# Softmax sums of fourteen heads in four column groups, and one reciprocal a head spread over the partitions through DRAM

## The chip, the cores and the metric

The kernel runs on all 8 cores of one Trainium2 chip. Each core does the same work on its own half of one of the four sequences. The metric is the time on the device in microseconds (us) of the slowest core; lower is better.

## What is computed

One transformer layer: attention with 16 heads of 128 columns over a sequence of 2048, a residual and a layer norm, then a feed-forward net of 8192 hidden columns, again with residual and layer norm. The part that the change touches is the softmax and its normalisation:

```python
q = (x @ Wq.T + bq).reshape(b, s, h, dh) * jnp.cos(rot)
k = (x @ Wk.T + bk).reshape(b, s, h, dh) * jnp.sin(rot)
v = (x @ Wv.T + bv).reshape(b, s, h, dh)
scores = jnp.einsum('bshd,bthd->bhst', q, k) / np.sqrt(dh) * spiral_weight[None, :, None, None]
attn = jax.nn.softmax(scores, axis=-1)
out = jnp.einsum('bhst,bthd->bshd', attn, v).reshape(b, s, d)
x = _layernorm(x + out @ Wo.T + bo)
x = _layernorm(x + gelu(x @ proj1.T + b1) @ proj2.T + b2)
```

Each core has 1024 queries (its half of the sequence) and all 2048 keys.

## The kernel before

Each engine has its own program, written out by hand, and the programs meet in semaphores. `H`, `X` and `W` are large tiles in SBUF in which named slices live; `ps` is all of PSUM, eight banks of 512 f32 columns, and `pair` is two double banks that the score steps use in turn.

The attention stage is a loop over 16 heads h with 16 steps tc each, one step for every 128 keys. In a step TensorE computes the scores of 128 keys against the 1024 queries into one `pair` (L658), then a share of projection matmuls as filler (L460 for k, L464 for q of the next head, L469 for v; `jobs(h)` is how many of these jobs of 16 matmuls a head has: 10 in heads 0 and 8 to 12, 9 in heads 1, 2 and 4 to 7, 8 in head 3, 7 in head 13, 5 in head 14), then the product of the exponentials of the step before with v (`p_v`, L607). ScalarE takes the exponential out of `pair` (L874) into one of three buffers, and VectorE adds it into `acc` (L1042). So `acc` holds, for each query, 128 partial sums, one on each partition; after the last step VectorE splits it into two bf16 halves, `hl` (L1057, L1059).

The sum over the partitions is `denom`, in step 2 of the next head: four matmuls with a stationary matrix of ones of 128 columns (L617), so that the total of each query comes out on every one of the 128 partitions. ScalarE copies this 128x1024 block to `rec` (`denom_out`, L852), VectorE takes its reciprocal in four pieces of 256 columns (`recip`, L993) in steps 3 to 6, and multiplies the head's output `avraw` with it in step 7 (`normalise`, L998). With two semaphores around it: TensorE goes on to step 4 of a head only when `a_den` tells that the copy is done, and ScalarE overwrites `avraw` at the start of the next head only when `d_norm` tells that the multiplication is done.

In step 12 of a head (13 in heads 3 and 13; `norm_step`) the bound of the next head's scores is worked out. TensorE adds squares in `norm_sums` (L479, L482), eight matmuls whose stationary matrix is 32 columns wide and which go to four groups of 32 partitions. VectorE takes maxima (`norm_pick`, L972 to L976) and sets `d_nsel`; TensorE spreads them one step later (`norm_all`, L489, which waits for `d_nsel`), VectorE multiplies (`norm_out`, L981, L986, sets `d_nprod`), TensorE waits for that before the scores of the step after, and GpSimd makes `neg_b` from it (L392, L394), which ScalarE needs for the next head's first exponential.

GpSimd issues all weight loads, with a conversion from f32 to bf16 under way (`load`, L371). Its program has a pass for each head h, which runs while TensorE is in head h-1: it waits for `pe_k`, loads wk for head h+2, waits for `pe_q`, loads wq for head h+1, waits for `d_nprod`, makes `neg_b`. Some passes end with loads of their own: pass 1 and 9 four slabs of wv, pass 12 and 13 four slabs of wo (`won`), pass 14 six slabs of wo, after it has waited for `pe_k` to reach 64, which is after the third job of head 14. SyncE moves the residual through DRAM meanwhile (`xpieces`, `xbo_scr`).

After the heads come the product with wo (L725), layer norm, the two products of the feed-forward net (L744, L755; L784, L800) and the last layer norm, whose statistics are in the tiles `ln_st`.

Of the kernel before, what the change touches and what calls it, by code (L numbers as in the profile page):

```python
# [89 lines left out]
def build():  # L90
# [15 lines left out]
    consts = nc.dram_tensor("consts", [128, 68], F32, kind="ExternalInput").ap()  # L106
    xbo_scr = nc.dram_tensor("xbo_scr", [1024, 2048], F32, kind="Internal").ap()
    x1_scr = nc.dram_tensor("x1_scr", [1024, 2048], F32, kind="Internal").ap()
    r2_scr = nc.dram_tensor("r2_scr", [1024, 512], F32, kind="Internal").ap()
    out = nc.dram_tensor("out", [1024, 2048], F32, kind="ExternalOutput").ap()  # L110

    with contextlib.ExitStack() as ctx:
# [15 lines left out]
        b2_bc = sbuf("b2_bc", [128, 2048], F32)  # L128

        bo_bc = sbuf("bo_bc", [128, 2048], F32)  # L130
        ln_st = [sbuf(f"ln_st{i}", [128, 24 if i < 7 else 30], F32) for i in range(8)]
        ln_mv = [sbuf(f"ln_mv{i}", [128, 2], F32) for i in range(8)]
        ln_cols = sbuf("ln_cols", [128, 24], F32)
        ln_sd, ln_rs, ln_nm = [[ln_cols[:, k * 8 + i:k * 8 + i + 1] for i in range(8)]
# [76 lines left out]
        s_bo = sem("s_bo")  # L211
        s_bv = [sem("s_bv0"), sem("s_bv1")]
        s_b2 = sem("s_b2")
        s_xt = [sem(f"s_xt{i}") for i in range(8)]
        s_x = [sem(f"s_x{i}") for i in range(16)]
        s_xp = [sem("s_xp0"), sem("s_xp1")]
# [31 lines left out]
        d_trig, d_const, d_v = sem("d_trig"), sem("d_const"), sem("d_v")  # L248
        d_nsel, d_nprod = sem("d_nsel"), sem("d_nprod")
        d_acc, d_hl, d_norm = sem("d_acc"), sem("d_hl"), sem("d_norm")  # L250
        d_xbo, d_r1 = sem("d_xbo"), sem("d_r1")
        d_mv1, d_x1bf = sem("d_mv1"), sem("d_x1bf")
        d_r2, d_mv2, d_nm2 = sem("d_r2"), sem("d_mv2"), sem("d_nm2")
# [114 lines left out]
        @block.gpsimd  # L368
        def _(e):
            def load(dst, src, done):  # L370
                e.dma_start(out=dst, in_=src, max_dma_last_dim=8192).then_inc(done, 16)  # L371

            for g in range(4):
                load(H[:, half(g, 2048)], xtc[g], s_x[g])
                load(wslab[2 + g], wvc[g], s_wv[g])
                load(H[:, half(4 + g, 2048)], xtc[4 + g], s_x[4 + g])
                load(wv1[g], wvc[4 + g], s_wv1[g])
            load(wk[0], wkt[0], s_wk[0])
            load(wslab[1], wqt[0], s_wq)
            for i in range(8, 16):  # L380
                load(H[:, half(i, 2048)], xtc[i], s_x[i])
            load(wk[1], wkt[1], s_wk[1])
            for h in range(16):
                if h < 15:
                    if h < 14:
                        e.wait_ge(pe_k, 4 * (h + 1))
                        load(wk[h % 2], wkt[h + 2], s_wk[h % 2])
                    e.wait_ge(pe_q, 2 * (h + 1))
                    load(wslab[1], wqt[h + 1], s_wq)

                e.wait_ge(d_nprod, h + 1)
                e.tensor_tensor(nroot[:], nprod[:], half_sb[:], ALU.pow).then_inc(g_root, 1)  # L392
                e.wait_ge(g_root, h + 1)
                e.tensor_single_scalar(neg_b[:, h:h + 1], nroot[:], -1.0,  # L394
                                       ALU.mult).then_inc(g_negb, 1)


                if h == 1:
                    e.wait_ge(pe_v, 24)
                    for g in range(4):  # L400
                        load(wslab[2 + g], wvc[8 + g], s_wv[g])
                if h == 9:
                    e.wait_ge(pe_v, 48)
                    for g in range(4):
                        load(wslab[2 + g], wvc[12 + g], s_wv[g])
                if h == 12:
                    e.wait_ge(pe_av, 192)
                    for d in range(4):
                        load(wo_sb[d], won[d], s_wo[d])
                if h == 13:  # L410
                    e.wait_ge(pe_v, 64)
                    for d in range(4, 8):
                        load(wo_sb[d], won[d], s_wo[d])
                if h == 14:
                    e.wait_ge(pe_k, 64)
                    for d in range(8, 14):
                        load(wo_sb[d], won[d], s_wo[d])
            e.wait_ge(pe_q, 32)
            for d in range(14, 16):
                load(wo_sb[d], won[d], s_wo[d])  # L420

            def slab(n, src):
                load(wslab[ring(n)], src, s_w[ring(n)])

            for n in range(2):
                slab(n, p1t[n])
            e.wait_ge(pe_av, 256)
            for i in range(2):
                load(p1_own[i], p1t[2 + i], s_own[i])
            e.wait_ge(pe_wo, 32)  # L430

            e.wait_ge(s_xt[7], 16)
            for n in range(4, 64):

                if 8 <= n < 10:
                    e.wait_ge(pe_f1, n - 7)
                elif n >= 10:
                    e.wait_ge(pe_f1, n - 5)
                slab(n, p1t[n])
            for n in range(60):  # L440
                if n < 6:
                    e.wait_ge(pe_f1, 59 + n)
                else:
                    e.wait_ge(pe_p2, n - 5)
                slab(G_P2 + n, p2n[n // 16][n % 16])
                if n == 57:

                    e.wait_ge(pe_p2, 52)
                    for i in range(4):
                        load(p2_late[i], p2n[3][12 + i], s_wl[i])  # L450
            for s in range(8):
                e.wait_ge(d_nm2, s + 1)
                e.tensor_scalar(r2[2][s], r2[2][s], ln_rs[s][:], ln_nm[s][:],
                                ALU.mult, ALU.add).then_inc(g_out, 1)
# [3 lines left out]
        def _(t):  # L458
# [153 lines left out]

            def denom(h, dst):
                t.wait_ge(d_hl, h + 1)
                for sc in range(2):
                    for part in range(2):
                        ins = t.matmul(dst[:, half(sc, 512)], ones_sq_sb[:],  # L617
                                       hl[:, half(2 * part + sc, 512)],
                                       start=(part == 0), stop=(part == 1))
                ins.then_inc(pe_den, 1)  # L620
# [185 lines left out]
        def _(a):  # L806
# [42 lines left out]

            def denom_out(h, src):  # L850
                a.wait_ge(pe_den, h + 1)
                a.activation(out=rec if h < 15 else rec15, in_=src, func=AF.Copy).then_inc(a_den, 1)  # L852


            a.wait_ge(d_v, 16)
# [76 lines left out]
        def _(v):  # L932
# [61 lines left out]

            def normalise(h):
                v.wait_ge(a_av, h + 1)
                v.drain()
                v.tensor_mul(pool_a[h], avraw if h < 15 else avraw15,  # L998
                             rec if h < 15 else rec15).then_inc(d_norm, 1)
# [28 lines left out]
            for h in range(16):  # L1028
                for tc in range(16):
                    n = 16 * h + tc  # L1030
                    if tc == norm_step(h) and h < 15:
                        norm_pick(h + 1, pair[(turn(h, tc) + 1) % 2])
                    if tc == norm_step(h) + 1 and h < 15:
                        norm_out(h + 1, pair[(turn(h, tc - 1) + 1) % 2])
                    if tc == 1:
                        v.wait_ge(a_exp, n + 1)
                        v.drain()
                        v.tensor_add(acc, pbuf[(n - 1) % 3], pbuf[n % 3]).then_inc(d_acc, 2)
                    if tc > 1:
                        v.wait_ge(a_exp, n + 1)  # L1040
                        v.drain()
                        v.tensor_add(acc, acc, pbuf[n % 3]).then_inc(d_acc, 1)  # L1042
                    if 0 < h < 15 and 3 <= tc <= 6:
                        recip(h - 1, tc - 3)
                    if 0 < h < 15 and tc == 7:
                        normalise(h - 1)
                    if 0 < h < 12 and tc in (1, 8, 10) and (h, tc) != (11, 10):
                        if h == 1 and tc == 1:
                            v.wait_ge(s_bo, 16)
                        add_bo(3 * h - 3 + (1, 8, 10).index(tc))  # L1050
                    for j in range(jobs(h)):
                        kind, c, blk = job(h, j)
                        if job_ends(h, j) == tc and kind == "v":
                            v_out(c, blk, JOB_BANK[kind, c, blk])
                    if tc == 15:
                        v.drain()
                        v.tensor_copy(hl[:, half(0)], acc)  # L1057
                        v.drain()
                        v.tensor_sub(hl[:, half(1)], acc, hl[:, half(0)]).then_inc(d_hl, 1)  # L1059
# [32 lines left out]
            for p in range(4):  # L1092
                r_p = r2a if p == 0 else r2[p]
                for s in range(8):
# [29 lines left out]
                    if p == 3:  # L1124
                        if s == 0:
                            v.wait_ge(s_r2r, 128)
                        v.drain()
                        v.bn_aggr(ln_mv[s][:], ln_st[s][:]).then_inc(d_mv2, 1)  # L1128
                        v.wait_ge(a_sd2, s + 1)
                        v.reciprocal(ln_rs[s][:], ln_sd[s][:])  # L1130
                        v.drain()
# [81 lines left out]
```

## Time and profile before

| | us |
|---|---|
| median of 3 runs | 1829.99 (1829.6 to 1830.45) |
| the profiled execution | 1830.17 |
| its span, slowest of 8 cores (core 5) | 1828.3 |
| spans of the 8 cores | 1825.9 to 1828.3 |
| TensorE busy | 1798.1 (98%) |
| VectorE busy | 711.5 (39%) |
| ScalarE busy | 536.4 (29%) |
| GpSimd busy | 143.4 (8%) |

The span is the time from the first to the last instruction of the core; a little lies around it. In the profile PE is TensorE (matmuls), PEld its weight loads, DVE VectorE, ACT ScalarE, POOL GpSimd, SP SyncE. A group or row names the line of the kernel, what it writes and reads (`out<-in`, without buffer numbers), and how often. A matmul's own duration (379 ns for 512 columns) is longer than the time that it takes in the stream, since matmuls are pipelined; the distance from one start to the next is what it costs. In brackets stands the idle time before an instruction and what ended it.

### The profile page before, as it was taken

Reading aid. Unit: us, or ns where it says so; the run is one execution under the profiler, and the core shown is the slowest. Engines: PE = TensorE matmul, PEld = TensorE weight load, DVE = VectorE, ACT = ScalarE, POOL = GpSimd, SP = SyncE. Lnnn points to the kernel's source line nnn. Section 1 sums busy time; section 2 is a strip of 40 time slices with the busy share of each in tenths; the row PEclk is TensorE's granted clock in tenths of the full one; section 3 lists DMA queues with packets and bytes.
Section 4 is the critical chain, followed back from the end, with each engine's and each line's share of the span. In section 5 each row is a group of like instructions: output and inputs, shape, how many; then the busy total and the mean of one; then the engine's idle time right before and its main releaser. Section 6 shows DMA issues by size and latency. Waiting matters only on the chain.

```text
span 1828.3 us, 22539 instructions; the slowest of 8 cores (1825.9 to 1828.3 us)
## 1 busy us (share of the span) xinstructions
PE 1798.1 (98%) x8448; PEld 814.5 (45%) x8448; DVE 711.5 (39%) x841; ACT 536.4 (29%) x539; POOL 143.4 (8%) x252
## 2 busy tenths in 40 slices
PE   6999999999999999999999999999999999999997
PEld 2444444444444444434444444444444444444444
DVE  5436777777666666688620000000000030210315
ACT  0135556555555555672211111111110000000001
POOL 3001000000000011010000000000000000000011
PEclk9999999999999999999999999999999999999999
DMA  9934323223253324375876544545544485565776
GB/s 162 161 71 76 61 56 67 55 56 61 59 99 60 53 38 62 57 115 152 230 165 112 81 73 77 79 73 80 75 75 70 75 161 88 95 106 76 156 128 177
DMA packets 70889, 172.45 MB, mean 94 GB/s; under 512 B 22912, under 2 KB 22912, under 8 KB 68480
## 3 DMA queue, kind: packets, MB, share of 16 engines
q0 software_dynamic: 29952, 109.07, 39.4%
q1 hardware_dynamic: 39680, 59.85, 12.6%
q10 hardware_dynamic: 1152, 2.10, 0.5%
q8 instruction: 71, 1.16, 0.3%
q14 instruction: 34, 0.28, 0.1%
HBM read 248.58 MB, written 27.26 MB: 151 GB/s over the span
## 4 chain that ended last, share of the span: by engine, by line
PE 97%; DMA 1%; ACT 1%; DVE 0%; issue 0%; DVEq 0%; POOL 0%; ACTq 0%; POOLq 0%
PE ps L784 24%; PE ps L755 23%; PE ps L469 12%; PE ps L460 12%; PE ps L464 6%; PE ps L607 6%; PE ps L658 6%; PE ps L725 5%; PE ps L744 2%; PE ps L627 1%; PE ps L617 1%; DMA W<-wvc 1%; ACT X L874 0%; PE ps L800 0%; DVE X L1042 0%
## 5 line engine op out<-in xcount | busy, mean ns | idle before, releaser
L755 PE MATMUL ps<-X,W 128*128 128x512 bf16 x1920 | 414.6, 379 | 0.0
L784 PE MATMUL ps<-W,H 128*128 128x512 bf16 x1904 | 412.1, 379 | 0.0
L874 ACT ACTIVATE X<-ps,neg_b 128x1024 bf16<-128x1024 f32 x256 | 284.5, 1112 | 242.1 <-PE ps L658 232.6
L1042 DVE TENSOR_TENSOR X<-X 128x1024 f32<-128x1024 f32 x224 | 274.4, 1225 | 180.1 <-ACT X L874 169.9
L755 PEld LDWEIGHTS ps<-X,W 128*128 128x128 bf16 x1920 | 187.8, 98 | 226.6
L784 PEld LDWEIGHTS ps<-W,H 128*128 128x128 bf16 x1904 | 186.3, 98 | 224.6
L1121 DVE TENSOR_TENSOR X<-ps,bo_bc 128x512 f32<-128x512 f32 x24 | 16.6, 691 | 662.0 <-PE ps L784 660.3
L469 PE MATMUL ps<-W,H 128*128 128x512 bf16 x768 | 188.9, 382 | 15.3 <-DMA W<-wvc 15.3
L917 ACT ACTIVATE H<-ps,b_sb 128x1024 bf16<-128x1024 f32 x64 | 71.3, 1114 | 353.1 <-PE ps L755 347.6
L607 PE MATMUL ps<-X,H 128*128 128x512 bf16 x512 | 152.2, 379 | 2.0 <-ACT X L874 1.7
L658 PE MATMUL ps<-X 128*128 128x512 bf16 x480 | 142.7, 379 | 0.5 <-DVE nprod L986 0.4
L464 PE MATMUL ps<-H,W 128*128 128x512 bf16 x512 | 130.3, 379 | 0.0
L460 PE MATMUL ps<-H 128*128 128x512 bf16 x512 | 129.6, 379 | 0.0
L460 PE MATMUL ps<-H,W 128*128 128x512 bf16 x512 | 127.8, 379 | 0.0
L469 PEld LDWEIGHTS ps<-W,H 128*128 128x128 bf16 x768 | 74.7, 99 | 105.9 <-issue 21.6
L921 ACT ACT_TABLE_LOAD x1 | 1.3, 1283 | 394.5 <-DVE ln_mv L1128 394.5
L993 DVE RECIPROCAL X<-X 128x256 f32<-128x256 f32 x60 | 104.3, 1743 | 0.0
L817 ACT ACTIVATE X<-ps,bks,sinv 128x512 bf16<-128x512 f32 x60 | 46.5, 775 | 110.2 <-PE ps L460 110.2
L607 PEld LDWEIGHTS ps<-X,H 128*128 128x128 bf16 x512 | 49.4, 98 | 64.8 <-issue 6.7
L464 PEld LDWEIGHTS ps<-H,W 128*128 128x128 bf16 x512 | 50.1, 98 | 60.4
L460 PEld LDWEIGHTS ps<-H,W 128*128 128x128 bf16 x512 | 50.1, 98 | 60.4
L460 PEld LDWEIGHTS ps<-H 128*128 128x128 bf16 x512 | 50.1, 98 | 60.0 <-issue 0.3
(119 smaller groups left out, 1081.4 us busy)
## 6 DMA issues: line engine op xcount, KB each, us to landing
W<-p1t POOLq DMA_DIRECT2D x62, 512.0 KB, 5.9
W<-p2n POOLq DMA_DIRECT2D x60, 512.0 KB, 8.5
H<-xtc POOLq DMA_DIRECT2D x16, 512.0 KB, 50.7
W<-wqt POOLq DMA_DIRECT2D x16, 512.0 KB, 7.8
xpieces<-xn SPq DMA_DIRECT2D x32, 256.0 KB, 3.9
xbo_scr<-xpieces SPq DMA_DIRECT2D x32, 256.0 KB, 4.3
H<-xbo_scr SPq DMA_DIRECT2D x8, 1024.0 KB, 7.1
x_scr<-H SPq DMA_DIRECT2D x8, 1024.0 KB, 4.9
```

The source lines that it names most:

```text
L460: return t.matmul(bank[b], wk[h % 2][:, half(i, 128)], x_t(c, i), start=(i == 0), stop=(i == 15))
L464: return t.matmul(bank[b], wslab[1][:, half(i, 128)], x_t(c, i), start=(i == 0), stop=(i == 15))
L469: return t.matmul(bank[b], x_t(blk // 4, i)[:, half(blk % 4, 128)], w[:, half(i % 4, 512)], start=(i == i0), stop=(i == i1 - 1))
L607: ins = t.matmul(bank[4 + sc], v_blk(h // 4, tc)[:, half(h % 4, 128)], pbuf[n % 3][:, half(sc, 512)], start=(tc == 0), stop=(tc == 15))
L658: ins = t.matmul(pair[k % 2][:, half(sc, 512)], kbuf[h][:, half(tc, 128)], qbuf[h % 2][:, half(sc, 512)], start=True, stop=True)
L725: ins = t.matmul(bank[(s % 2) * 4 + c], pool_a[d][:, half(s, 128)], wo_sb[d][:, half(c, 512)], start=(d == 0), stop=(d == 15))
L755: ins = t.matmul(bank[b0 + c], wslab[ring(ho)][:, half(i, 128)], X[:, i * 1024 + c * 512:i * 1024 + (c + 1) * 512], start=(i == 0), stop=( ...
L784: ins = t.matmul(bank[s], hid[k][:, half(s, 128)], w[:, half(i, 512)], start=(k == 0), stop=(k == (31 if p == 3 and s == 7 else 63)))
L874: a.activation(out=pbuf[n % 3], in_=pair[turn(h, tc) % 2], func=AF.Exp, bias=neg_b[:, h:h + 1]).then_inc(a_exp, 1)
L917: a.activation(out=hid[ho], in_=ps[:, half(ho % 4)], func=AF.Gelu, bias=b1_sb[:, ho:ho + 1]).then_inc(a_gelu, 1)
L993: v.reciprocal(r[:, half(i, 256)], r[:, half(i, 256)])
L1042: v.tensor_add(acc, acc, pbuf[n % 3]).then_inc(d_acc, 1)
```

## The change

The sums of the heads 0 to 13 are computed another way; heads 14 and 15 stay as they were. `denom` now gives eight matmuls of 256 columns with a stationary matrix of 32 columns: the queries 256c to 256c+255 are summed into the partitions 32c to 32c+31, first for one half of `hl`, then for the other. So each total stands on 32 partitions and not on 128, and the block is 128x256. ScalarE copies this block into a new tile `rec4`. VectorE takes one reciprocal of it, in step 3, and sets `d_rec`.

GpSimd waits for that at the top of its pass h, from pass 2 on, for the reciprocals of head h-2. It issues a write of one row of each group (partitions 0, 32, 64, 96; 4 rows of 1 KB) to a DRAM tensor `rec_scr`, waits until it has landed, and issues a read of these 4 KB, broadcast to all 128 partitions, into `rec` (512 KB). `normalise` waits for this transfer (`s_rec`) and is moved from step 7 to step 11. The statistics `ln_st` of the layer norms, which were tiles of their own, now lie in `rec4`.

```diff
+        rec4 = sbuf("rec4", [128, 256], F32)
+        ln_st = [rec4[:, i * 24:i * 24 + (24 if i < 7 else 30)] for i in range(8)]
...
             for h in range(16):
+
+                if h >= 2:
+                    e.wait_ge(d_rec, h - 1)
+                    e.dma_start(out=rec_scr[:], in_=rec4[0:128:32, :]).then_inc(s_rst, 16)
+                    e.wait_ge(s_rst, 16 * (h - 1))
+                    e.dma_start(out=rec, in_=rec_scr.rearrange("a b -> (a b)").unsqueeze(0)
+                                .to_broadcast([128, 1024])).then_inc(s_rec, 16)
                 if h < 15:
                     if h < 14:
                         e.wait_ge(pe_k, 4 * (h + 1))
...
             def denom(h, dst):
                 t.wait_ge(d_hl, h + 1)
+                if h < 14:
+
+                    for part in range(2):
+                        for c in range(4):
+                            ins = t.matmul(dst[32 * c:32 * c + 32, 0:256], ones_sq_sb[:, 0:32],
+                                           hl[:, half(4 * part + c, 256)],
+                                           start=(part == 0), stop=(part == 1))
+                    ins.then_inc(pe_den, 1)
+                    return
...
             def denom_out(h, src):
                 a.wait_ge(pe_den, h + 1)
-                a.activation(out=rec if h < 15 else rec15, in_=src, func=AF.Copy).then_inc(a_den, 1)
+                if h < 14:
+                    a.activation(out=rec4[:], in_=src[:, 0:256], func=AF.Copy).then_inc(a_den, 1)
+                else:
+                    a.activation(out=rec if h < 15 else rec15, in_=src,
+                                 func=AF.Copy).then_inc(a_den, 1)
...
             def normalise(h):
                 v.wait_ge(a_av, h + 1)
+                if h < 14:
+                    v.wait_ge(s_rec, 16 * (h + 1))
                 v.drain()
...
-                    if 0 < h < 15 and 3 <= tc <= 6:
-                        recip(h - 1, tc - 3)
-                    if 0 < h < 15 and tc == 7:
+                    if 0 < h < 15 and tc == 3:
+                        v.wait_ge(a_den, h)
+                        v.reciprocal(rec4[:], rec4[:]).then_inc(d_rec, 1)
+                    if 0 < h < 15 and tc == 11:
                         normalise(h - 1)
```

## Rows read from the trace of the kernel before

**Rows 1.** The page's first part: busy us (share), instructions.

```profile
PE 1798.1 (98%) x8448; PEld 814.5 (45%) x8448; DVE 711.5 (39%) x841; ACT 536.4 (29%) x539; POOL 143.4 (8%) x252
```

**Rows 2.** Windows, head 14: length, PE, PEld, DVE, ACT, POOL busy; PEclk, DMA share, GB/s.

```profile
769.30:806.00 36.70, 34.62 (x165) 15.24 (x164) 28.52 (x27) 25.09 (x28) 4.67 (x8) 1.00 0.48 75
```

**Rows 3.** TensorE's waits in the span: us in total, times, longest us.

```profile
PE ps L469 <- DMA W<-wvc: 15.3, 1, 15.3
```

**Rows 4.** Timeline of TensorE, the sums in head 1: start us, us, what.

```profile
163.23 1.03 PE L617 MATMUL ps<-b_bc,ones_sq_sb 128*128 128x512 bf16 x4
164.09 0.38 PE L460 MATMUL ps<-H,W 128*128 128x512 bf16 x1
```

**Rows 5.** Timeline of TensorE, norm_sums in step 12 of head 1.

```profile
191.72 0.59 PE L658 MATMUL ps<-X 128*128 128x512 bf16 x2
192.24 0.40 PE L479 MATMUL ps<-b_bc,ones_sq_sb 128*32 128x512 bf16 x4
192.47 0.28 PE L482 MATMUL ps<-X,ones_sq_sb 128*32 128x256 bf16 x4
192.69 1.04 PE L469 MATMUL ps<-H 128*128 128x512 bf16 x4
```

**Rows 6.** Groups by line, each shape apart: busy us, mean ns, idle before.

```profile
L993 DVE RECIPROCAL X<-X 128x256 f32<-128x256 f32 x60 | 104.3, 1743 | 0.0
L998 DVE TENSOR_TENSOR H<-X 128x1024 bf16<-128x1024 f32 x15 | 18.4, 1225 | 1.4
```

**Rows 7.** Timeline, all engines: nsel and norm_all of heads 1 and 11.

```profile
194.11 0.22 DVE L976 TENSOR_SCALAR nsel<-consts_sb,nmax 128x4 f32<-128x4 f32 x1
...
195.50 0.28 PE L489 MATMUL ps<-nsel,onesf_sb 128*128 128x8 f32 x2
...
668.00 0.23 DVE L976 TENSOR_SCALAR nsel<-consts_sb,nmax 128x4 f32<-128x4 f32 x1
...
669.61 0.28 PE L489 MATMUL ps<-nsel,onesf_sb 128*128 128x8 f32 x2
```

**Rows 8.** Timeline of GpSimd in head 14: the loads that end pass 14.

```profile
786.45 3.25 POOL L371 DMA_DIRECT2D H<-won  x6 [16.85 <-PE ps L460]
```

**Rows 9.** The page's third part: packets, MB and share of the software queue.

```profile
q0 software_dynamic: 29952, 109.07, 39.4%
```

**Rows 10.** DMA issues of 786.4 to 786.9 and 789.1 to 789.7: median us to landing.

```profile
H<-won POOLq DMA_DIRECT2D x1, 512.0 KB, 6.8
...
H<-won POOLq DMA_DIRECT2D x2, 512.0 KB, 19.2
```

**Rows 11.** The tile won, all 16 loads of it.

```profile
DMA to landing us min/median/max: 6.5/11.8/20.1
```

**Rows 12.** DMA issues of SyncE: constants and broadcasts at 0, 210, 839 us.

```profile
b_bc<-bvr SPq DMA_DIRECT2D x2, 256.0 KB, 8.0
consts_sb<-consts SPq DMA_DIRECT2D x1, 34.0 KB, 1.9
...
b_bc<-bvr SPq DMA_DIRECT2D x1, 256.0 KB, 4.7
...
b_bc<-b2r SPq DMA_DIRECT2D x1, 1024.0 KB, 8.1
```

**Rows 13.** Timeline, all engines: norm_pick and norm_all in head 14.

```profile
801.45 0.68 DVE L972 TENSOR_REDUCE nmax<-ps 128x1 f32<-128x512 f32 x1
...
802.68 0.22 DVE L976 TENSOR_SCALAR nsel<-consts_sb,nmax 128x4 f32<-128x4 f32 x1
...
803.05 0.36 PE L489 MATMUL ps<-nsel,onesf_sb 128*128 128x8 f32 x2 [0.62 <-DVE nsel L976]
```

**Rows 14.** Windows: the first matmuls of the run, which begin at 15.3 us.

```profile
16.00:20.00 4.00, 4.00 (x12) 1.42 (x11) 1.38 (x2) 0.00 (x0) 0.00 (x0) 1.00 1.05 167
```

**Rows 15.** DMA issues of 730.6 to 731.2: the end of pass 13.

```profile
W<-won POOLq DMA_DIRECT2D x2, 512.0 KB, 14.8
```

**Rows 16.** Timeline of VectorE: the addition of step 11 in head 13.

```profile
759.58 1.23 DVE L1042 TENSOR_TENSOR X<-X 128x1024 f32<-128x1024 f32 x1 [1.12 <-ACT X L874]
```

More of the change, by code:

```diff
@@ L108, in build @@
     x1_scr = nc.dram_tensor("x1_scr", [1024, 2048], F32, kind="Internal").ap()
+    rec_scr = nc.dram_tensor("rec_scr", [4, 256], F32, kind="Internal").ap()
     r2_scr = nc.dram_tensor("r2_scr", [1024, 512], F32, kind="Internal").ap()
@@ L130, in build @@
         bo_bc = sbuf("bo_bc", [128, 2048], F32)
-        ln_st = [sbuf(f"ln_st{i}", [128, 24 if i < 7 else 30], F32) for i in range(8)]
+        rec4 = sbuf("rec4", [128, 256], F32)
+        ln_st = [rec4[:, i * 24:i * 24 + (24 if i < 7 else 30)] for i in range(8)]
         ln_mv = [sbuf(f"ln_mv{i}", [128, 2], F32) for i in range(8)]
@@ L213, in build @@
         s_b2 = sem("s_b2")
+        s_rst, s_rec = sem("s_rst"), sem("s_rec")
         s_xt = [sem(f"s_xt{i}") for i in range(8)]
@@ L250, in build @@
         d_acc, d_hl, d_norm = sem("d_acc"), sem("d_hl"), sem("d_norm")
+        d_rec = sem("d_rec")
         d_xbo, d_r1 = sem("d_xbo"), sem("d_r1")
@@ L1127, in _ @@
                         v.drain()
-                        v.bn_aggr(ln_mv[s][:], ln_st[s][:]).then_inc(d_mv2, 1)
+                        v.bn_aggr(ln_mv[s][:], ln_st[s]).then_inc(d_mv2, 1)
                         v.wait_ge(a_sd2, s + 1)
```

## The prediction

> **What bounds the kernel now.** I read the page's busy shares first, then the windows of the attention stage, then who waits for whom, then the timeline around each line that the change touches, and last the landing times of the transfers around them. TensorE is busy 98% of the span [rows 1]. So time changes only if TensorE's own stream gets shorter, or if TensorE is made to wait. In head 14 TensorE is busy 34.62 of 36.70 us [rows 2]: that head has few projection jobs between its score steps, its cover is thin, and 2.08 us of waits already show there. The only wait of TensorE for a DMA in the whole execution is the one before the first matmul, 15.3 us [rows 3].
>
> **TensorE's part: shorter sums, 14 times.** Before, a head's four full-width matmuls of 512 columns occupy the stream from 163.23 to 164.09, that is 0.86 us, 0.215 each [rows 4]. Afterwards it is two rounds of four matmuls of 256 columns, each round on four column groups. The trace has that form in norm_sums [rows 5]. The last full-width pair starts at 191.72, so its two slots of 0.215 end at 192.15. The first group matmul starts at 192.24: 0.09 to enter. The round of 4 x 512 columns takes 192.24 to 192.47, 0.23 us, so the groups do run side by side. The round of 4 x 256 columns and the return to full width take 192.47 to 192.69, 0.22 us. The new sum is then 0.09 + 0.23/2 + 0.22 = 0.42 us, saving 0.44 us; 14 x 0.44 = 6.2 us. Bounds: at worst it costs as much as the whole of norm_sums, which is also eight matmuls, 0.54 us (saving 4.5 us); at best it costs its 2 x 0.108 us of columns and two thirds of the 0.22 us of entering and leaving that norm_sums shows below, 0.36 us (saving 7.0 us). In the full heads TensorE runs without a gap, so the saving moves everything behind it.
> Of the 0.54 us of norm_sums its columns at 0.215 per 512 explain 0.32 when the groups run side by side; 0.22 is entering and leaving the grouped form [rows 5]. The Trainium skill, TensorEngine Tiling (Array Packing), section Theoretical Speedup, promises up to 4x for a small dimension of 32, and its Key Properties warn that a change of tiling mode drains the engine; by the bare 4x the sum would be 0.22 us a head and the saving 9.0 us, by the row, where the drain shows, it is less, and the row decides.
>
> **VectorE and ScalarE parts.** Three of the four reciprocals of a head go, 3 x 1.743 us [rows 6], and ScalarE's copy shrinks to a quarter. Both lie beside TensorE's work: worth nothing on the path. What is moved is normalise, 1.225 us [rows 6], from step 7 to step 11, directly ahead of norm_pick at step 12 (step 13 in heads 3 and 13). Queued behind it are norm_pick, the addition of step 12 and norm_out; TensorE's norm_all waits for nsel. In the heads with nine jobs (1, 2, 4 to 7) nsel is ready at 194.11 + 0.22 = 194.33 and norm_all starts at 195.50 [rows 7]: slack 1.17. Normalise adds 1.225 + about 0.05 of drain, and a semaphore another 0.15 (nsel done at 802.90, norm_all at 803.05 [rows 13]), so norm_all comes about 0.25 us late: 6 x 0.25 = 1.5 us, bounds 0 and 2 (a third more). In the heads with ten jobs (8 to 12) the slack is 669.61 - 668.23 = 1.38 [rows 7], and normalise, drain and semaphore together ask for 1.43: at most 0.05 us each, counted as nothing. Heads 3 and 13 have a step in between.
>
> **GpSimd's part: two more transfers a head, in its own order.** At the top of its pass h (which runs while TensorE is in head h-1) GpSimd now waits for the reciprocal of head h-2, issues a 4 KB write, waits for it to land, and issues a 512 KB broadcast. Behind these are queued the loads of wk and wq, the power of nprod and neg_b. For most heads this is free: the reciprocal is ready after step 3, about 3 us times 8 before step 11 needs the result, and write and broadcast alone are 1.9 us or less and 4.7 to 8.1 us [rows 12]. After a batch of four loads it still is. The worst of these is the batch of pass 13: of its four transfers the last two, issued at 730.1 and 730.7, land 14.8 us later on average [rows 15], the last by about 746.5, and normalise's place in head 13 is 759.58 + 1.23 = 760.8 [rows 16]. Write and broadcast take about 8 us of these 14.
>
> Pass 15 is different, and it is what decides my forecast. Before it GpSimd is still in pass 14, waiting for pe_k = 64; from 786.45 to 789.70 it issues six loads of won [rows 8]. All GpSimd transfers are in one queue, q0: its 109.07 MB [rows 9] are just the 208 slab loads of 0.524 MB. These loads land one after another: the first 6.8 us after its issue, the fifth and sixth 19.2 on average [rows 10], the longest of all 20.1 us [rows 11]; that the longest is this sixth is my reading, and the fifth then took 18.3. The sixth is issued at 789.70 - 0.54 = 789.16, so it lands at 809.3. The write of head 13's reciprocals is issued at 789.8, behind them. The chain, in the clock of the run before:
> - write lands 0 to 1.9 us after the sixth load (the 34 KB constants took 1.9 us from their issue [rows 12]); this is smaller and already queued, I take 1.0: 810.3;
> - GpSimd sees it, 0.2, and issues the broadcast. A broadcast of 256 KB took 4.7 us, one of 1024 KB 8.1 us [rows 12]; by interpolation 512 KB is about 5.8, and I take 6.0 for the software queue: 816.5;
> - VectorE, standing in normalise of step 11 of head 14 since about 801.5, drains and multiplies, 1.35: 817.9;
> - norm_pick, which ran from 801.45 to 802.90 [rows 13], 1.45 + 0.05: 819.4; norm_all follows 0.15 later: 819.55.
> It started at 803.05 [rows 13]. TensorE can't pass it: the stall is 16.5 us, with the ends 809.3 + 0 + 4.7 and 809.3 + 1.9 + 8.1 giving 14.2 and 19.5. Nothing later gives it back: no later wait of TensorE is for a DMA [rows 3], and the loads behind keep their distance. What is next behind it (d_nprod, neg_b, head 15) keeps its distance from nsel.
> After such a gap the matmuls may run slowly at first: after the idle start only 12 lie in the window from 16 to 20 us [rows 14], though the granted clock reads 1.00 there. 4 us hold 18.6 slots of 0.215 us: 6.6 x 0.215 = 1.4 us. I take 1.4, bounds 0 and 2.
>
> **The sum.** The profiled execution took 1830.17 us (span 1828.3), 0.18 above the median of 1829.99. 1830.0 - 6.2 + 1.5 + 16.5 + 1.4 = 1843.2. Its own ends: 1830.0 - 7.0 + 0 + 14.2 + 0 = 1837.2, and 1830.0 - 4.5 + 2 + 19.5 + 2 = 1849.0.
>
> **Rivals.**
> A. The write doesn't queue behind the six loads, but shares the DMA engines with them. For it: the hardware queue's 256 KB broadcasts at the start got through in 8.0 us while q0 was loading, instead of 4.7 [rows 12]. Against: both new transfers are issued by GpSimd, all of whose transfers are in q0 [rows 9]. Write 3 us and broadcast 5.8 x 8.0/4.7 = 10 us: 789.8 + 3 + 0.2 + 10 = 803.0, norm_all at 806.0, a stall of 3 us (8 if the write takes 8): 1830.0 - 6.2 + 1.5 + 3 to 8 = 1828.3 to 1833.3, middle 1831.
> The landings of the six show order within q0 [rows 10]. The Trainium skill, DMA: Bandwidth & Descriptors, section SWDGE vs HWDGE vs iDMA, says that one software queue is allocated and that a DMA engine takes turns only between queues; by that the wait is whole, and case A would need a second queue.
> B. The broadcast is there before VectorE comes to it, 801.5: a gain on the other side. It decides from the moment that the broadcast lands before 801.5; it needs write and broadcast to be done within the 11.7 us from 789.8, with the DMA engines loaded. Then 1830.0 - 6.2 + 1.5 = 1825.3. Against it speak the landings in that stretch [rows 10, 11].
> C. The column groups don't help in this form (two accumulating rounds, the second waiting for the first): sums cost 0.86 as before, and the stall stays: 1843.2 + 6.2 = 1849.4.
> D. More heads are late than head 13, behind the batches of four loads in passes 2, 10, 13 and 14: each has about 6 us in hand, so this needs transfers twice as long; one more stall of 3 us or so gives 1846 or more.
>
> **How the numbers follow.** Forecast 0.76; A 0.10; B 0.05; C 0.04; D 0.05. About 0.2% (3.7 us) is what a measurement of this kernel can tell from no change: 1826.3 to 1833.7. B is faster, and a tip of A: 0.06. Most of A is within: 0.08. The rest is slower: 0.86. The range reaches from 1835 (below the forecast's own end, towards A) to 1850 (it takes in C and the ends).
>
> **What the profile would show.** TensorE's row of the sum as 4 + 4 matmuls of 128x256 within 0.42 us. One reciprocal of 1.74 us a head. In head 14 a wait of normalise of some 15 us for a DMA, ended by the broadcast into rec; TensorE idle before norm_all as long; GpSimd between six loads and the broadcast doing nothing for 20 us. Small waits of norm_all for nsel, 0.2 to 0.3 us, in six heads. I am wrong if TensorE has no gap above 5 us in head 14; then the order in q0 is the step that failed.

## The result and the profile after

The changed kernel is slower: 1.0062 times the kernel before, with a 95% interval of 1.0051 to 1.0074. On the 1830.1 us of before that is 1841.4 us (1839.4 to 1843.6). The forecast was 1843.2.

In three of its eight runs, the profiled one among them (there the cores 4 to 7), half of the cores ran at a lower granted clock than the others and took longer, so the median of all eight, 1842.38, is a little high, and all rows of after are of core 0, beside which before's core 0 has a span of 1827.4 us. First the spans and granted clocks of the cores, then TensorE's waits (us in total, times, longest):

```profile
core 0: 1839.3 us, clock 0.994
...
core 4: 1967.8 us, clock 0.924
```

```profile
PE ps L502 <- DVE nsel L1002: 16.5, 3, 16.1
PE ps L482 <- DMA W<-wvc: 15.1, 1, 15.1
```

The second row is the start, which was there before [rows 3]. The first is new: norm_all (now L502) waits for nsel, once for 16.1 us. Before, the wait at this place was 0.62 us [rows 13].

The timeline of core 0 in head 14, all engines, shows how it comes about:

```profile
797.03 0.60 PE L680 MATMUL ps<-X 128*128 128x512 bf16 x2
...
805.53 0.58 POOL L395 DMA_DIRECT2D X<-rec_scr  x1 [20.09 <-DMA rec_scr<-rec]
810.94 1.23 DVE L1026 TENSOR_TENSOR H<-X 128x1024 bf16<-128x1024 f32 x1 [14.21 <-DMA X<-rec_scr]
...
813.31 0.22 DVE L1002 TENSOR_SCALAR nsel<-consts_sb,nmax 128x4 f32<-128x4 f32 x1
...
813.68 0.57 PE L502 MATMUL ps<-nsel,onesf_sb 128*128 128x8 f32 x2 [16.06 <-DVE nsel L1002]
814.10 1.01 PE L649 MATMUL ps<-H 128*128 128x512 bf16 x2
814.91 1.06 PE L620 MATMUL ps<-X,H 128*128 128x512 bf16 x2
```

Read it backwards. TensorE stood still until nsel; nsel was made right behind normalise (L1026); normalise waited 14.2 us for the broadcast; and GpSimd (L395) had waited 20.1 us for its 4 KB write before it could issue the broadcast. GpSimd's own timeline has what stood in front of the write, the six loads of [rows 8]:

```profile
781.65 3.25 POOL L377 DMA_DIRECT2D H<-won  x6 [16.42 <-PE ps L473]
784.84 0.61 POOL L393 DMA_DIRECT2D rec_scr<-rec  x1
```

And the DMA issues of core 0 at 784.8 to 785 and at 805.5 (KB each, us from issue to landing). The sixth load, issued at about 784.3, lands at 804.8, the write, issued at 784.84, at 805.0:

```profile
H<-won POOLq DMA_DIRECT2D x1, 512.0 KB, 20.5
rec_scr<-rec POOLq DMA_DIRECT2D x1, 4.0 KB, 20.2
...
X<-rec_scr POOLq DMA_DIRECT2D x1, 512.0 KB, 5.3
```

The matmul pairs behind the gap last 1.01 and 1.06 us instead of 0.59. The windows of core 0 (length, busy of PE, PEld, DVE, ACT, POOL, then granted clock, DMA share, GB/s) show why:

```profile
799.00:813.00 14.00, 0.00 (x0) 0.00 (x0) 2.06 (x3) 0.00 (x0) 0.58 (x1) 0.55 0.42 95
...
815.00:817.00 2.00, 2.00 (x6) 0.62 (x5) 1.44 (x2) 0.08 (x1) 1.56 (x1) 0.50 0.00 0
817.00:819.00 2.00, 2.00 (x10) 0.90 (x9) 0.81 (x1) 1.49 (x2) 1.57 (x5) 0.91 0.00 0
819.00:821.00 2.00, 2.00 (x11) 0.91 (x10) 1.61 (x2) 1.82 (x3) 0.90 (x2) 1.00 0.79 92
```

TensorE was idle through the first of them, and the granted clock fell to its lower level (0.50, 1.2 GHz). It came back to 2.4 GHz within the window 817 to 819. From 813.7 to some 817.4 the matmuls ran at half rate, which would cost half of 3.7 us, about 1.9 us, in a stream without a gap. Here it costs less, since at the full rate TensorE has to wait for nprod in this stretch (0.39 us in before). The starts show the price: from norm_all to the first pair of score matmuls that reads xpieces it is 5.47 us in after (819.15, the first row below, less 813.68), and 4.34 in before (the other rows), both on core 0. The slow matmuls cost core 0 1.1 us; on cores 1 to 3 the same distance is 5.3 to 6.7 us.

```profile
819.15 0.60 PE L680 MATMUL ps<-X,xpieces 128*128 128x512 bf16 x2
...
803.21 0.36 PE L489 MATMUL ps<-nsel,onesf_sb 128*128 128x8 f32 x2 [0.62 <-DVE nsel L976]
...
804.97 0.59 PE L658 MATMUL ps<-X 128*128 128x512 bf16 x2 [0.39 <-DVE nprod L986]
...
807.55 0.59 PE L658 MATMUL ps<-X,xpieces 128*128 128x512 bf16 x2
```

The shorter sums are where they were expected, in TensorE's timeline of head 1 (beside [rows 4]). The pair before ends its two slots at 162.25 + 0.43 = 162.68, the next full-width matmul starts at 163.11, so the sum costs 0.43 us instead of 0.86:

```profile
162.25 0.60 PE L680 MATMUL ps<-X 128*128 128x512 bf16 x2
162.78 0.40 PE L632 MATMUL ps<-b_bc,ones_sq_sb 128*32 128x256 bf16 x8
163.11 1.04 PE L473 MATMUL ps<-H,W 128*128 128x512 bf16 x4
```

And the small price of the moved normalise, 32 us later in the same head (beside [rows 7], where norm_all stood right behind its pair):

```profile
194.10 0.59 PE L680 MATMUL ps<-X 128*128 128x512 bf16 x2
194.69 0.36 PE L502 MATMUL ps<-nsel,onesf_sb 128*128 128x8 f32 x2
194.90 1.02 PE L482 MATMUL ps<-H 128*128 128x512 bf16 x4
```

From the pair to norm_all it is 0.59 us instead of 0.43, and from there to the next 0.21 instead of 0.14: 0.23 us a head. The list of waits gives nsel only 16.5 us in three waits and doesn't name these, since a matmul's modelled end covers them; the distances of the starts do.

### The profile page after: what moved, and what is told of

It reads as the page before. It is cut to its first block, busy times and chain, and to the rows that moved or that the text cites. A ratio compares the mean times of both kernels' runs of the same rounds, so it can differ in the third digit from the quotient of the medians.

```text
span 1994.5 us, 22637 instructions; the slowest of 8 cores (1836.2 to 1994.5 us)
## 1 busy us (share of the span) xinstructions
PE 1952.8 (98%) x8504; PEld 847.2 (42%) x8504; DVE 642.8 (32%) x799; ACT 528.3 (26%) x539; POOL 159.3 (8%) x280
## 4 chain that ended last, share of the span: by engine, by line
PE 97%; DMA 2%; DVE 0%; ACT 0%; issue 0%; POOL 0%; DVEq 0%; ACTq 0%; POOLq 0%
PE ps L806 22%; PE ps L777 21%; PE ps L482 14%; PE ps L473 13%; PE ps L620 6%; PE ps L477 6%; PE ps L680 6%; PE ps L747 4%; PE ps L766 1%; PE ps L649 1%; DMA rec_scr<-rec 1%; DMA W<-wvc 1%; PE ps L822 0%; PE ps L492 0%; ACT X L900 0%; PE ps L632 0%
## 5 line engine op out<-in xcount | busy, mean ns | idle before, releaser
L806 PE MATMUL ps<-W,H 128*128 128x512 bf16 x1904 | 412.1, 379 | 0.0
L806 PEld LDWEIGHTS ps<-W,H 128*128 128x128 bf16 x1904 | 186.3, 98 | 224.6
L482 PE MATMUL ps<-W,H 128*128 128x512 bf16 x768 | 225.9, 439 | 16.6 <-DMA W<-wvc 16.6
L620 PE MATMUL ps<-X,H 128*128 128x512 bf16 x512 | 176.0, 430 | 1.5 <-ACT X L900 1.1
L680 PE MATMUL ps<-X 128*128 128x512 bf16 x480 | 166.5, 433 | 0.0
L477 PE MATMUL ps<-H,W 128*128 128x512 bf16 x512 | 153.9, 433 | 0.0
L473 PE MATMUL ps<-H,W 128*128 128x512 bf16 x512 | 152.9, 436 | 0.0
L473 PE MATMUL ps<-H 128*128 128x512 bf16 x512 | 152.3, 431 | 0.0
L482 PEld LDWEIGHTS ps<-W,H 128*128 128x128 bf16 x768 | 82.8, 110 | 133.6 <-issue 133.5
L620 PEld LDWEIGHTS ps<-X,H 128*128 128x128 bf16 x512 | 54.6, 108 | 80.7 <-issue 75.5
L477 PEld LDWEIGHTS ps<-H,W 128*128 128x128 bf16 x512 | 55.3, 108 | 77.6 <-issue 73.8
L473 PEld LDWEIGHTS ps<-H,W 128*128 128x128 bf16 x512 | 54.9, 108 | 78.4 <-issue 78.4
L473 PEld LDWEIGHTS ps<-H 128*128 128x128 bf16 x512 | 54.3, 108 | 76.2 <-issue 70.8
L680 PEld LDWEIGHTS ps<-X 128*128 128x128 bf16 x480 | 52.0, 108 | 73.0 <-issue 69.6
```

What stands on the lines that cost most here:

```text
L473: return t.matmul(bank[b], wk[h % 2][:, half(i, 128)], x_t(c, i), start=(i == 0), stop=(i == 15))
L477: return t.matmul(bank[b], wslab[1][:, half(i, 128)], x_t(c, i), start=(i == 0), stop=(i == 15))
L482: return t.matmul(bank[b], x_t(blk // 4, i)[:, half(blk % 4, 128)], w[:, half(i % 4, 512)], start=(i == i0), stop=(i == i1 - 1))
L620: ins = t.matmul(bank[4 + sc], v_blk(h // 4, tc)[:, half(h % 4, 128)], pbuf[n % 3][:, half(sc, 512)], start=(tc == 0), stop=(tc == 15))
L680: ins = t.matmul(pair[k % 2][:, half(sc, 512)], kbuf[h][:, half(tc, 128)], qbuf[h % 2][:, half(sc, 512)], start=True, stop=True)
L806: ins = t.matmul(bank[s], hid[k][:, half(s, 128)], w[:, half(i, 512)], start=(k == 0), stop=(k == (31 if p == 3 and s == 7 else 63)))
```

## The experiments

The theory: head 13's write stands in one queue behind six loads, and normalise, waiting for it, stands in front of norm_pick. Its rivals: the transfers are too slow for the short head 14 in any order; the DMA engines are full, whatever the queue; the broadcasts cost something in every head. The kernel before took 1830.4 us on the chip of e1 to e4, 1830.6 on that of e5 to e7, 1831.0 on that of e8 and e9.

**Write and broadcast ahead of the six loads.** Nothing is taken away: the same transfers, the same loads.

```diff
-                if h >= 2:
+                if 2 <= h < 15:
...
                 if h == 14:
+                    e.wait_ge(d_rec, 14)
+                    e.dma_start(out=rec_scr[:], in_=rec4[0:128:32, :]).then_inc(s_rst, 16)
+                    e.wait_ge(s_rst, 16 * 14)
+                    e.dma_start(out=rec, ...).then_inc(s_rec, 16)
                     e.wait_ge(pe_k, 64)
```

> All of the change, but GpSimd does head 13's wait, write and broadcast in pass 14, ahead of its wait for pe_k 64 and the six loads of won. Queue-order theory: write and broadcast are done before the first load has landed, the gap of TensorE before norm_all in head 14 (16.1 us) is gone with its slow matmuls, and what stays is 14 sums at 0.43 us less and 6 heads at 0.23 us more: 1830.1 - 6.0 + 1.4 = 1825.5 us. Rival, head 14 is too short for the two transfers wherever they stand: normalise still waits some us for the broadcast, 1829 us or more.

Measured: 1828.9 us, ratio 0.9991 (0.9982 to 0.9999). The long wait is gone and with it 12.5 us or so; the kernel is now slightly faster than the one before (the interval ends just below 1), but 3.4 us above what I expected. The rival's number was 1829 or more, so the time alone doesn't tell it from the theory; the timeline does. Its timeline (core 7; GpSimd first, then VectorE and TensorE in head 14) shows it, and what the rest is:

```profile
779.88 0.61 POOL L429 DMA_DIRECT2D rec_scr<-rec  x1 [13.32 <-DVE rec L1078]
782.18 0.58 POOL L431 DMA_DIRECT2D X<-rec_scr  x1 [1.69 <-DMA rec_scr<-rec]
782.99 3.18 POOL L377 DMA_DIRECT2D H<-won  x6 [0.23 <-issue]
...
798.16 1.23 DVE L1031 TENSOR_TENSOR H<-X 128x1024 bf16<-128x1024 f32 x1
...
800.91 0.36 PE L507 MATMUL ps<-nsel,onesf_sb 128*128 128x8 f32 x2 [1.94 <-DVE nsel L1007]
...
802.66 1.01 PE L685 MATMUL ps<-X 128*128 128x512 bf16 x2 [0.39 <-DVE nprod L1017]
```

The write lands in 1.7 us when nothing stands before it, and normalise (798.16) has no wait for the broadcast, against the rival. But normalise in step 11 holds nsel back by its own 1.3 us even when it waits for nothing (1.94 us of wait instead of 0.62), and the matmuls behind run slowly again, though the wait was only 2 us. The window from 796 to 812 has it at 0.89 on all eight cores; here core 0:

```profile
796.00:812.00 16.00, 13.95 (x63) 0.89 0.85 145
```

0.11 of 16 us is at most about 1.7 us. From norm_all to the pair that reads xpieces it is 5.5 to 6.0 us on the eight cores, where before has 4.34: 1.1 to 1.7 us. In the sum of the prediction the 1.3 us was hidden inside the chain after the broadcast; in the expectation of this run I left it out, and the clock too.

**Step 9 in the heads with nine jobs.** `tc == (9 if jobs(h) == 9 else 11)` for normalise, on top of the edit above.

> As e1_rec_before_loads, and normalise stands in step 9 instead of 11 in the heads with nine jobs (1, 2, 4 to 7). If normalise just ahead of norm_pick costs 0.23 us in each of these six heads, 1.4 us less than e1_rec_before_loads: 1824.1 us. If the two are the same, that term is nothing. Rival: the broadcast isn't there by step 9 in head 1, where four loads of wvc stand before it; then VectorE falls behind and it is slower than e1_rec_before_loads.

Measured: 1825.84 us, 0.9975 (0.9966 to 0.9985), 3.1 us below the run before it. That is more than the 1.4 expected. In this run's profile the granted clock from 796 to 812 reads 1.00 on seven cores and 0.89 on core 2 alone, although norm_all waits 1.9 us here too. So up to 1.7 us of the gain is the clock; core 2 loses 1.0 us to it (5.35 us from norm_all to the pair that reads xpieces) and is the longest, at 1823.7 us. The rival would have made it slower. What decides on which cores a gap of this size costs the clock, these runs don't tell.

**Head 13 as before, all others changed.** `h < 14` becomes `h < 13` in `denom`, `denom_out` and `normalise`; for head 13 the four reciprocals in steps 3 to 6 and normalise in step 7; no transfers in pass 15.

> The change for heads 0 to 12; head 13 as before (full-width sums, four reciprocals, normalise in step 7, no transfers). Queue-order theory: only head 13's transfers stall, so the whole loss is gone: 1830.1 - 13 x 0.43 + 1.4 = 1825.9 us. Rival, the broadcasts cost a little in every head: 1830 us or more.

Measured: 1826.67 us, 0.9979 (0.9970 to 0.9987). The expected time was 1825.9, so the thirteen other heads with their 26 transfers cost nothing that this measurement can tell (its interval is 1.6 us to either side); the loss is in head 13 alone. norm_all waits 0.62 us in head 14 and the clock stays at 1.00.

**The moved step alone, in the kernel before.** `tc == 11` instead of `tc == 7` for normalise, nothing else.

> The kernel before, with one edit: normalise in step 11 instead of 7. It measures the term of the moved step alone: 6 x 0.23 = 1.4 us more, 1831.5 us, with norm_all late by 0.15 to 0.25 us in six heads and in head 14 by up to 1.3 us more, since there norm_all already waited for nsel; with that, 1832.9 us. Rival, it is hidden: 1830.1 us.

Measured: 1834.19 us, 1.0021 (1.0012 to 1.0029), so 3.8 us more. By the sum 1.4 is the nine-job heads and 1.3 head 14, which leaves 1.1. The clock reads 0.89 in the window from 796 to 812 on four of the eight cores, and there the stretch behind norm_all is 1.4 to 1.7 us longer than in before. That this makes the rest isn't shown: the longest core of the profiled execution, core 3 with 1832.2 us, is one at 1.00, and 1.1 us is less than the interval of 1.5 to either side.

**Head 13 changed, all others as before.** The conditions turned round.

> The change for head 13 alone; all other heads as before. Queue-order theory: the whole stall with one head's gain, 1830.1 - 0.4 + 16.1 of waiting + 1.9 of slow matmuls after it = 1847.7 us; GpSimd waits 20 us for its 4 KB write. Rival, the stall needs the traffic of all fourteen heads: about 1830 us.

Measured: 1845.37 us, 1.0083 (1.0065 to 1.0100). One head's transfers are enough for the whole loss. It is 2.3 us below the expected number, which took the 16.1 us wait of core 0 of after; here norm_all waits 12.9 to 15.2 us on the eight cores. Timeline of core 1:

```profile
789.72 0.61 POOL L393 DMA_DIRECT2D rec_scr<-rec  x1
810.69 0.58 POOL L395 DMA_DIRECT2D X<-rec_scr  x1 [20.36 <-DMA rec_scr<-rec]
...
817.66 0.57 PE L502 MATMUL ps<-nsel,onesf_sb 128*128 128x8 f32 x2 [15.16 <-DVE nsel L1002]
```

**Three loads before the write, three after the broadcast.** `range(8, 11)` in pass 14, `range(11, 14)` in pass 15 behind the broadcast.

> All of the change, but only three of the six loads of won stand before head 13's write; the other three are issued after the broadcast. Queue-order theory: the write lands three loads of 3.3 us earlier, the stall is 16.1 - 9.8 = 6.3 us, and the time 1842.4 - 9.8 = 1832.6 us, or 1 us less if the clock recovers faster after the shorter gap. Rival, the wait is a matter of a busy DMA subsystem and not of order: the loads behind the broadcast now run beside it, and the time stays near 1842 us.

Measured: 1834.19 us, 1.0020 (1.0008 to 1.0032). Timeline of core 0:

```profile
784.53 0.59 POOL L393 DMA_DIRECT2D rec_scr<-rec  x1
796.95 0.57 POOL L395 DMA_DIRECT2D X<-rec_scr  x1 [11.83 <-DMA rec_scr<-rec]
...
806.03 0.57 PE L505 MATMUL ps<-nsel,onesf_sb 128*128 128x8 f32 x2 [7.16 <-DVE nsel L1005]
```

The write lands 11.9 us after its issue instead of 20.2, TensorE waits 7.2 us instead of 16.1. The wait goes with the number of loads in front of it, 2.8 us of landing a load (8.3 for three). The time is 1.6 us above my number: the wait of core 0 fell by 8.9 and not 9.8, and the remaining 0.7 is within the interval. The cores differ here: norm_all waits 3.6 to 3.8 us on cores 1, 3 and 7 and 6.0 to 7.2 on the others, and the profiled execution, with 1832.0 us, is the shortest of this kernel. The slow matmuls are behind the shorter waits too.

**The same moment, another queue.** SyncE issues head 13's two transfers, after a signal from GpSimd behind its six loads, and normalise of head 13 waits for the second of them. Pass 15 has none.

```diff
                     for d in range(8, 14):
                         load(wo_sb[d], won[d], s_wo[d])
+                    e.tensor_single_scalar(sig[:], half_sb[:], 1.0, ALU.mult).then_inc(g_sig, 1)
...
@@ SyncE, ahead of its wait for pe_v 64
+            e.wait_ge(g_sig, 1)
+            e.wait_ge(d_rec, 14)
+            e.dma_start(out=rec_scr[:], in_=rec4[0:128:32, :]).then_inc(s_rst2, 16)
+            e.wait_ge(s_rst2, 16)
+            e.dma_start(out=rec, ...).then_inc(s_rec2, 16)
```

> All of the change, but head 13's write and broadcast are issued by SyncE, on its own queue, after a signal that GpSimd gives when it has issued its six loads: the same moment, the same DMA engines busy, another queue. Queue-order theory: the write lands in 2 to 5 us instead of 20, the broadcast takes 6 to 10 beside the loads, normalise waits 0 to 5 us, and the time is 1826 to 1831 us. Rival, the DMA engines are simply full: the write still takes 15 us or more, 1840 us.

Measured: 1834.41 us, 1.0023 (1.0011 to 1.0034). First two rows of the timeline of core 4 (SP's queue), two rows of it in head 14, then the broadcast among the DMA issues:

```profile
786.61 0.63 SPq L319 DMA_DIRECT2D rec_scr<-rec  x1
793.27 0.32 SPq L321 DMA_DIRECT2D X<-rec_scr  x1
...
804.26 1.22 DVE L1038 TENSOR_TENSOR H<-X 128x1024 bf16<-128x1024 f32 x1 [6.21 <-DMA X<-rec_scr]
...
807.00 0.57 PE L512 MATMUL ps<-nsel,onesf_sb 128*128 128x8 f32 x2 [8.05 <-DVE nsel L1012]
```

```profile
X<-rec_scr SPq DMA_DIRECT2D x1, 512.0 KB, 10.9
```

With the same loads under way, SyncE's write is done within the 6.7 us between its two issues (5.2 to 7.0 on the eight cores), against 20.2 in GpSimd's queue: it was order behind GpSimd's loads that held it. The run changes the issuing engine together with the queue, so it doesn't tell whether this order is kept in the queue itself or on GpSimd's way to it. And the rival is not nothing. A 4 KB write that takes 1.7 us alone took up to 6.7 beside the loads, and the broadcast 10.9 instead of about 5.5. Those 11 us were still too long for head 14, and I had given the write 2 to 5 us; with normalise's own 1.3 us and the slow matmuls behind a wait of 8 us the time came out 3 us above my range. The Trainium skill, DMA: Bandwidth & Descriptors, section Issuing engines are not separate DMA queues, says that transfers of all issuing engines run on the same 16 DMA engines and interleave; the 10.9 us agree.

**Head 14's normalise in step 9.** On top of e1's edit: `tc == (9 if h == 14 else 11)`.

> As e1_rec_before_loads, and in head 14 normalise stands in step 9 instead of 11; the heads with nine jobs keep step 11. Theory after seven runs: in e1_rec_before_loads normalise holds nsel back 1.3 us in head 14 and the slow matmuls after that wait cost 1.7 us, so this is 3.0 us below its 1828.9: 1825.9 us, norm_all waits 0.6 us for nsel as before and the granted clock stays 1.00 on all cores. Rival, the slow matmuls come from something else in that stretch: only 1.3 us less, 1827.6 us.

Measured: 1826.16 us, 0.9975 (0.9964 to 0.9985). That is 2.7 us below e1, or 3.3 when each is taken from its own before; 3.0 was expected, 1.3 by the rival. TensorE's row in head 14 (core 1) is that of before again, and the window reads 1.00 on all eight cores (here core 0), against the rival. From norm_all to the pair that reads xpieces it is 4.34 us again:

```profile
799.82 0.36 PE L507 MATMUL ps<-nsel,onesf_sb 128*128 128x8 f32 x2 [0.62 <-DVE nsel L1007]
```

```profile
796.00:812.00 16.00, 14.60 (x73) 1.00 1.01 164
```

**Step 9 in all those heads.** On top of e1's edit: `tc == (9 if jobs(h) in (5, 9) else 11)`; head 14 is the one with five jobs.

> As e8_step9_h14, and step 9 in the heads with nine jobs too. All that is left of the change is then the shorter sums: 14 x 0.43 = 6.0 us below the kernel before, 1824.4 us, and 1.4 us below e8_step9_h14. If it is the same as e8_step9_h14, the term of the nine-job heads was nothing and e2_norm_step9 gained by the clock alone.

Measured: 1824.23 us, 0.9963 (0.9950 to 0.9977): the lowest ratio of all, though its interval overlaps those of e2 and e8, and 6.7 us below before (1831.0), where 6.0 were expected. The nine-job heads gave 1.9 us (1.4 expected, within what the two intervals allow). In head 1 norm_all stands right behind its pair again, 0.44 us after it (core 1):

```profile
195.47 0.59 PE L685 MATMUL ps<-X 128*128 128x512 bf16 x2
195.91 0.28 PE L507 MATMUL ps<-nsel,onesf_sb 128*128 128x8 f32 x2
```

## Why the prediction was right

By its own terms, against core 0 of after and the runs:

| term | predicted us | measured us | by |
|---|---|---|---|
| fourteen sums | -6.2 | -6.0 | 0.43 a head in the timeline; e9: -6.7 in all (-4.2 to -9.2) |
| normalise ahead of norm_pick, six heads | +1.5 | +1.4 to 1.9 | 0.23 a head; e8 less e9: 1.9 |
| stall of norm_all in head 14 | +16.5 | +15.4 | norm_sums to norm_all: 813.68 - 795.71 = 17.97, before 2.53 |
| slow matmuls behind it | +1.4 | +1.1 | norm_all to the pair that reads xpieces: 5.47, before 4.34 |
| sum | +13.2 | +11.9 | spans of core 0: +11.9 (1839.3 - 1827.4); runs: +11.3 (9.3 to 13.5) |

The chain of the stall held link by link. Counted from the issue of the six loads: the sixth load after 23.2 us (predicted 22.9); the write 0.2 us behind it (predicted 1.0, bounds 0 to 1.9); the broadcast's issue 0.5 us later (predicted 0.2, for which no row was given); its landing 5.3 us (6.0); normalise, norm_pick and norm_all 2.9 us (3.0). The mis-sized links are the write and the broadcast, each 0.7 or so too long; they are most of the difference between 16.5 and 15.4. The waits of norm_all on cores 1, 2 and 3 were 15.8, 14.0 and 13.6 us; core 0 had the longest.

That the order in q0 is what held the write was the step I named as the one to fail. It held: moving the transfers ahead of the loads (e1), leaving head 13 out (e3), changing it alone (e5), and halving the loads in front (e6) all moved the time as this order says, and another queue (e7) got the write through in a third of the time. Rival A, that write and loads share the DMA engines, is shown wrong for the kernel as changed. As a cost of its own, its mechanism is real, and e7 measures it. Rival B, a broadcast in time, is what e1 makes of it, though at 1828.9 and not at its 1825.3, for the reasons that follow. C and D did not happen: the sums cost 0.43 us in the accumulating form, and the reciprocals of head 12, behind a batch of four loads, were multiplied at 756.5 on core 0, where no wait is listed.

Two things I had not seen. The moved normalise costs 1.3 us in head 14 whatever the DMA does, because norm_all had no slack there before [rows 13]; I had counted it only in the heads with nine jobs, and it lay unseen inside the stall. And the clock term is not tied to a long stall: it came with a 2 us wait as well, and that, with the 1.3 us, is why e1 was above its number.

The slow matmuls were taken from the start of the run, where the granted clock read 1.00 in the windows in which they were few [rows 14]. Behind the stall it reads 0.50. The row that I took the term from doesn't show the same thing, and I read it too low: its 32 matmuls, from 15.30 to 24.27, take 8.97 us instead of 6.88, which is 2.1 us lost and not 1.4. That the term came out near core 0's 1.1 us is luck. Why the start is slow at 1.00 stays open.

## What to carry to other kernels

A small transfer that somebody waits for costs what stands before it in its queue: look up the last batch that its issuing engine sent, and put the small transfer ahead of it, or on another queue, knowing that there it still shares the DMA engines (here the first gave 0.9991 and the second 1.0023). When a step on a side engine is moved, look for the nearest place behind it where the bounding engine already waits with no slack; there the moved step counts in full. Here the same idea with two moves (transfers ahead of the loads, normalise in step 9) gave 0.9963 instead of 1.0062.

## What the runs showed of the hardware

- A wait of TensorE of 1.9 us, with waits of 0.8 and 0.3 us shortly ahead of it, was followed by matmuls at 1.2 GHz: mean granted clock 0.89 over 16 us, 1.0 to 1.7 us lost by the starts. It came on eight cores of eight in e1, four in e4 and one in e2 (a wait of 1.9 us in each). With the 0.62 us wait of before, e3, e8 and e9 it came on none.
- A 4 KB write took 1.7 us (median of 14 in after, the first thirteen 1.6 to 4.3), 20.2 behind six loads in its queue, 11.9 behind three, and at most 5.2 to 7.0 beside six on another queue. A 512 KB broadcast took 5.5 us (median in after, 4.7 to 7.0) and 10.3 to 11.2 beside the loads in e7.
- Four column groups of 32 with 2 x 256 columns took 0.43 us, where full-width matmuls took 0.86. Of the 0.43, 0.22 is columns at 0.215 per 512, 0.10 lies before the first of them (162.68 to 162.78), and 0.11 between the rounds or behind them, which the rows don't separate.
